# Delta rule: where three steps stand in the order of a pair of heads

## The reference, cut to what matters

```
conv = silu(conv1d(q, k, v))                    # 4 taps, per channel
decay = exp(tril(g_i - g_j))                    # g: sums of the gates in the chunk
tri = tril(k_beta @ k.T * decay, -1)
Tm = inverse(eye + tri)
v_new = Tm @ v_beta;  k_cum = Tm @ (k_beta * exp(g))
# over the chunks, one after the other:
v_n = v_new - k_cum @ S
out = q * exp(g) @ S + (q @ k.T * decay) @ v_n
S = S * exp(g_last) + (k * exp(g_last - g)).T @ v_n
# then per head
h = rmsnorm(out) * norm_weight * silu(z);  y = h @ W_out
```

## Time and profile before

| | before |
|---|---|
| median of the runs shown | 3314.37 us |
| the profiled execution, its own time | 3316.07 us |
| its span, first to last instruction | 3314.3 us |
| PE / weight load / VectorE / ScalarE / GpSimd busy | 91 / 63 / 70 / 37 / 31% |
| mean granted TensorE clock | 0.96 of full speed |

### The profile page before, as it was taken

The page is one execution under the profiler, slowest core; times in us unless marked ns, Lnnn a source line. Parts: engine busy times, 40 slices in busy tenths (PEclk is TensorE's granted clock), DMA queues, the critical chain, the costliest instruction groups (busy, mean ns, idle before and its releaser), DMA issues. The chain is left out here.

```text
span 3314.3 us, 81973 instructions
## 1 busy us (share of the span) xinstructions
PE 3003.8 (91%) x33019; PEld 2075.3 (63%) x33019; DVE 2307.2 (70%) x5231; ACT 1222.2 (37%) x2943; POOL 1022.4 (31%) x1495
## 2 busy tenths in 40 slices
PE   6999999599987999989999989999999999998897
PEld 3444444256655677677667767767776776776565
DVE  4666677778865776776776776777677677676466
ACT  2343333233333433343343343344344334332354
POOL 2454555348852221222221221221222122121011
PEclk8999999699988999999999999999999999998899
DMA  2111111000011110010010010000001001000000
GB/s 80 40 51 33 33 29 33 14 1 1 1 28 29 43 34 18 18 31 21 17 31 18 21 31 18 21 23 26 21 18 30 18 21 30 18 18 2 2 26 26
DMA packets 94040, 80.43 MB, mean 24 GB/s; under 512 B 54992, under 2 KB 68320, under 8 KB 93664
## 3 DMA queue, kind: packets, MB, share of 16 engines
q1 hardware_dynamic: 93664, 75.18, 8.4%
HBM read 57.70 MB, written 4.85 MB: 19 GB/s over the span
## 5 line engine op out<-in xcount | busy, mean ns | idle before, releaser
L1814 PE MATMUL gd_bk<-gd_xT,gd_wh 128*128 128x512 f32 x768 | 398.1, 628 | 22.1 <-DVE gd_L L1582 14.2
L480 DVE TENSOR_REDUCE at_nm<-at_ring 128x2 f32<-128x256 f32 (+3 forms) x256 | 199.2, 820 | 144.6 <-PE at_ring L623 144.6
L1528 DVE SCALAR_TENSOR_TENSOR gd_YK<-gd_bk,gd_cw,gd_YK 128x511 f32<-128x511 f32 (+2 forms) x384 | 282.8, 742 | 11.8 <-ACT gd_YK L1401 6.2
L1586 DVE COPY_PREDICATED gd_U<-gd_mU,gd_bk 128x256 f32<-128x256 int32 x320 | 140.9, 442 | 209.3 <-PE gd_bk L2016 149.5
L1994 PE MATMUL gd_bk<-gd_L,gd_NT 64*64 64x64 f32 x5120 | 212.5, 225 | 64.0 <-DVE gd_L L1588 41.3
L2011 PE MATMUL gd_bk<-gd_U,gd_ZS 64*64 64x64 f32 x5120 | 211.3, 225 | 39.4 <-ACT gd_ZS L1494 39.3
L1483 ACT COPY gd_O<-gd_bk 64x128 f32<-64x128 f32 x448 | 108.6, 260 | 356.9 <-PE gd_bk L1952 355.9
L1994 PEld LDWEIGHTS gd_bk<-gd_L,gd_NT 64*64 64x64 f32 x5120 | 177.9, 137 | 97.4 <-DVE gd_L L1588 55.8
L1494 ACT COPY gd_ZS<-gd_bk 128x256 f32<-128x256 f32 x320 | 115.2, 370 | 328.2 <-PE gd_bk L1994 324.9
L2011 PEld LDWEIGHTS gd_bk<-gd_U,gd_ZS 64*64 64x64 f32 x5120 | 178.4, 138 | 85.4 <-ACT gd_ZS L1494 43.5
L302 POOL TENSOR_TENSOR at_PT<-at_PT,at_dm 128x1024 f32<-128x1024 f32 (+3 forms) x128 | 198.0, 1547 | 10.7
(11 more groups left out here) (353 smaller groups left out, 6922.2 us busy)
## 6 DMA issues: line engine op xcount, KB each, us to landing
gd_wh<-in_L_attn_W_qkvz SPq DMA_DIRECT2D x64, 512.0 KB, 3.6
gd_gb<-gates SPq DMA_DIRECT2D x128, 64.0 KB, 3.3
X<-in_L_attn_x SPq DMA_DIRECT2D x8, 512.0 KB, 8.7
at_QT<-at_QS SPq DMA_DIRECT2D x128, 32.0 KB, 2.0
at_KT<-at_KS SPq DMA_DIRECT2D x128, 32.0 KB, 2.0
at_OC<-at_Ob SPq DMA_DIRECT2D x128, 32.0 KB, 2.0
at_RC<-inverse SPq DMA_DIRECT2D x128, 32.0 KB, 1.8
out_x<-X SPq DMA_DIRECT2D x8, 512.0 KB, 2.9
```

What stands on the lines that cost most here:

```text
L480: nc.vector.tensor_reduce(nm[v % 2][:, k, c0:c0 + HS + 1:HS], set_of(s, 2 + p)[:, :, 0:n], AX.X, ALU.max).then_inc(max_done, 1)
L1528: nc.vector.scalar_tensor_tensor(out[:, s:W], bank_[:, 0:W - s], cw[:, j, head(f, e), CONVK - 1 - s:CONVK - s], out[:, s:W], ALU.mult, ALU ...
L1586: last = nc.vector.copy_predicated(U[e][:, :, :], wide(mU[l]), chunks(A_[e], 1))
L1814: ins = nc.tensor.matmul(out[:, :], wh[e][:, k, col * DK:(col + 1) * DK], xT[:, k, :], start=k == 0, stop=k == DC - 1)
```

## The change

Seven moves and one new instruction in `delta_rule`; nothing else is changed.

1. ScalarE: `decays` of both heads go from level 1 to step 5, behind the first tap of head 0's values. A new Silu of one column (`warm`) stands in step 6 behind the copies to O and ahead of the squares. The first tap of head 1's values goes from step 6 to step 7.
2. GpSimd: `exponents(f + 1)` goes ahead of the gate weights (now a function of their own) and the key scales.
3. VectorE: head 1's first masked level in step 7 stands ahead of the output additions, in a new `front_middle`.
4. PE: the query projection of head 0 goes from the end of step 7 to step 8, behind the output products.
5. VectorE: the scalings of the outputs go from level 2, one behind each head's copies, to level 3, both ahead of the copies; the query taps of head 1 from level 3 to level 4.
6. PE and ScalarE: the heads' transposes and copies go from level 3 to level 4, `queries_out` of head 1 from level 4 to level 5; the values' transposes from level 4 to level 3.
7. PE: the output projection, four parts, goes from levels 4 and 5 to level 5 (one part) and behind it (three).

```diff
--- before.py
+++ after.py
@@ -973,6 +973,7 @@
         mL = [sb(f"mL{l}", [P, CK], I32) for l in range(LEVELS - 1)]
         xT = sb("xT", [P, DC, W])
         mhalf = sb("mhalf", [P, 2 * TPS])
+        warm = sb("warm", [P, 1])
         gates = nc.dram_tensor("gates", (NT * H, P), F32, kind="Internal").ap()
         glast = nc.dram_tensor("glast", (NT * H, CPT), F32, kind="Internal").ap()
         bk = [[bank(f"bk{e}{i}") for i in range(4)] for e in E2]
@@ -1308,6 +1309,8 @@
                         ge(pool, kc_mm[e], f)
                         nc.gpsimd.tensor_copy(U[e][:, :, :], wide(identc))
                         nc.gpsimd.tensor_copy(L[e][:, :, :], wide(identc)).then_inc(ui_done[e], 1)
+                def gate_weights(f):
+
                     for e in E2:
                         pool.wait_ge(z_silu[e], f + 1)
                         nc.gpsimd.tensor_tensor(zz[e][f % 2][:, :, :], zz[e][f % 2][:, :, :],
@@ -1382,9 +1385,11 @@
                     f = q + 1
                     if has(f):
                         prepare(f)
-                        key_scales(f)
                     if has(f + 1):
                         exponents(f + 1)
+                    if has(f):
+                        gate_weights(f)
+                        key_scales(f)
                     if ends_seq(q - 1):
                         row_scales(seq(q - 1))
                     if has(q):
@@ -1462,8 +1467,13 @@
                     if n == 3:
                         keys_out(f, 1)
                         gate_out(f, 1)
-                    if n in (5, 6):
-                        values_first(f, n - 5)
+                    if n == 5:
+                        values_first(f, 0)
+                        if has(f + 1):
+                            decays(f + 1, 0)
+                            decays(f + 1, 1)
+                    if n == 7:
+                        values_first(f, 1)
                     if n == 8:
                         queries_first(f, 0)
 
@@ -1481,6 +1491,8 @@
                                 act.wait_ge(p1_mm[e], q * RS + m)
                                 ge(act, ht_mm[e], q)
                                 nc.scalar.copy(O[e][rows(c), t, :], A_[e][rows(1 - c), 0:DK]).then_inc(o1_done[e], 1)
+                        if has(f) and n == 6:
+                            nc.scalar.activation(warm[:, :], mhalf[:, 0:1], ACT.Silu)
                         if has(q) and n >= 2 and n % 2 == 0:
                             squares(q, 0, n // 2 - 1)
                         if has(q) and n >= 2 and n % 2 == 0:
@@ -1494,18 +1506,15 @@
                                 nc.scalar.copy(ZS[e][:, :, :], chunks(A_[e])).then_inc(zs_done[e], 1)
                         if l == 1 and has(f):
                             queries_first(f, 1)
-                            if has(f + 1):
-                                decays(f + 1, 0)
-                                decays(f + 1, 1)
                             values_out(f, 0)
                         if l == 2 and has(f):
                             values_out(f, 1)
-                        if l == 3 and has(q):
+                        if l == 3 and has(f):
+                            queries_out(f, 0)
+                        if l == 4 and has(q):
                             heads_out(q, 0)
                             heads_out(q, 1)
-                        if l == 3 and has(f):
-                            queries_out(f, 0)
-                        if l == 4 and has(f):
+                        if l == 5 and has(f):
                             queries_out(f, 1)
                         if l == 5 and ends_seq(f) and has(f + 1):
                             act.wait_ge(xt_mm, DC * (seq(f) + 1) + 1)
@@ -1694,6 +1703,10 @@
                     if n == 7:
                         first_level(f, 0)
 
+                def front_middle(f, n):
+                    if n == 7:
+                        first_level(f, 1)
+
                 def front_late(f, n):
                     if n == 0:
                         keys_tap(f, 0, 1)
@@ -1711,8 +1724,6 @@
                         lower(f, 0)
                     if n == 6:
                         values_tap(f, 0, 1)
-                    if n == 7:
-                        first_level(f, 1)
                     if n == 8:
                         values_tap(f, 0, 2)
                         values_tap(f, 0, 3)
@@ -1747,6 +1758,8 @@
                                         dve.wait_ge(egl_in, 16)
                                     nc.vector.scalar_tensor_tensor(S[e][:, :], S[e][:, :], egl_row[:, col:col + 1], A_[e][:, DK:2 * DK],
                                                                    ALU.mult, ALU.add).then_inc(s_done[e], 1)
+                        if has(f):
+                            front_middle(f, n)
                         for e in E2:
                             m = n
                             if has(q) and 0 <= m < NCH and m % CPT == CPT - 1:
@@ -1770,7 +1783,10 @@
                         if l == 2 and has(f):
                             for s in range(1, CONVK):
                                 queries_tap(f, 0, s)
-                        if l == 3 and has(f):
+                        if l == 3 and has(q):
+                            heads_scaled(q, 0)
+                            heads_scaled(q, 1)
+                        if l == 4 and has(f):
                             for s in range(1, CONVK):
                                 queries_tap(f, 1, s)
                         if l == 5 and has(f):
@@ -1779,8 +1795,6 @@
                         for e in E2:
                             if has(f):
                                 level(f, e, l)
-                            if l == 2 and has(q):
-                                heads_scaled(q, e)
                         if l in (4, 5):
                             n = 2 * (f - FIRST_TERN) + l - 4
                             if 0 <= n < FSTEPS + PSTEPS:
@@ -1919,6 +1933,8 @@
                         values_in(f, 1, 1)
                     if n == 7:
                         lower_across(f, 1)
+                    if n == 8:
+                        queries_in(f, 0)
 
                 def front_late(f, n):
                     if n == 0:
@@ -1937,8 +1953,6 @@
                         values_in(f, 1, 0)
                     if n == 6:
                         lower_across(f, 0)
-                    if n == 7:
-                        queries_in(f, 0)
 
                 x_in(0, 0)
                 x_in(0, 1)
@@ -1996,13 +2010,13 @@
                                 last.then_inc(z_mm[e], 1)
                         if l == 1 and has(f):
                             queries_in(f, 1)
-                        if l == 3 and has(q):
+                        if l == 3 and has(f):
+                            values_across(f, 0)
+                        if l == 4 and has(q):
                             heads_across(q, 0)
                             heads_across(q, 1)
-                        if l == 4 and has(f):
-                            values_across(f, 0)
-                        if l >= 4 and ends_seq(q):
-                            project_out(seq(q), 2 * l - 8)
+                        if l == 5 and ends_seq(q):
+                            project_out(seq(q), 0)
                         for e in E2:
                             if has(f):
                                 pe.wait_ge(zs_done[e], f * (LEVELS - 1) + l)
@@ -2016,10 +2030,11 @@
                                             last = nc.tensor.matmul(A_[e][rows(c), t * CK:(t + 1) * CK], U[e][rows(c), t, :], ZS[e][rows(c), t, :],
                                                                     start=True, stop=True)
                                 last.then_inc(y_mm[e], 1)
-                        if l == 4 and has(f):
+                        if l == 3 and has(f):
                             values_across(f, 1)
-                        if l >= 4 and ends_seq(q):
-                            project_out(seq(q), 2 * l - 7)
+                        if l == 5 and ends_seq(q):
+                            for t in range(1, TPS):
+                                project_out(seq(q), t)
                     if ends_seq(f) and has(f + 1):
                         for e in E2:
                             ge(pe, ht_out[e], q + 1)
```

## The result

| | before | after |
|---|---|---|
| median of the runs | 3314.35 us | 3192.78 us |
| lowest to highest | 3314.29 to 3314.68 | 3184.38 to 3195.21 |
| the profiled execution | 3316.07 us, span 3314.3 | 3194.53 us, span 3192.8 |
| mean granted TensorE clock | 0.96 | 0.965 |

The ratio is 0.963, with an interval from 0.9614 to 0.9645: 121.6 us faster, where 100 were forecast. The direction and the mechanism hold, but the size was forecast too small. The changed kernel also spreads over 11 us between its runs, the one before over 0.4 us here.

A forecast was written before the change was run, and what follows sets the result against it. PE bounds the kernel, so only its waits can go: 23 ordinary pairs 75.9, seven sequence starts 20.3, with first and last pairs 99.7 us, giving 3214 us; own range 3195 to 3232, wide range 3192 to 3248 (0.80).

The forecast's parts named there:

- What bounds the kernel: PE, busy 3003.8 of 3314.3 us; only its waits can go, 115.4 us in four kinds around the inverse's levels.
- The exponentials in step 5: ScalarE: load and exponentials, 2.02 us, fit step 5 with 0.6 us spare; second load behind step 6's copies; cost nothing.
- the drain of the Trainium skill: ScalarE's table switches: 1.38 us drain atop 1283 ns, 2.66 us a switch; by it some 57 us above the forecast sum.
- GpSimd and the transfers: GpSimd's mask and G additions go ahead of gate weights, ending near 1831.1, about 17 us earlier; nothing lost.
- The rival on the slower side: Exponentials reach step 5 before their input, delaying ScalarE's copies and the recurrence; 25 us lateness gives 3491 us; chance 0.03.
- The rival of costlier switches: ScalarE's loads each hold it 2.57 us, making step 6's and 7's copies late: 52 us back, 3266; chance 0.03.
- The first masked level: VectorE does head 1's before the output additions in step 7; PE's waits of 0.45 and 0.71 us go.
- The levels, followed anew: Retimed levels 1 to 5 of one pair: 3.3 of PE's 4.12 us of waits go, 0.8 stay.
- The sum's check from totals: PE's four wait kinds, 115.4 us, less 0.8 for each of 32 pairs, is 90; some 10 us more missing there.
- The clock: Granted clock in the delta rule, mean 0.98: 10 us possible each way, none taken.
- VectorE as the bound: Rival: scalings and taps ahead of the level copies expose 1.13 us a pair, 34 us: 3248; chance 0.12.
- No change: Rival: PE's waits are only handed on to what ends last in the recurrence: 3314; chance 0.02.

The follow-up runs named there:

- the third kernel: Only the moves within the levels (scalings, query taps, transposes and copies, output projection), on the kernel before: 3293.7 us, ratio 0.9937.

## Why the prediction was right and wrong, point by point

- *What bounds the kernel.* Right: PE's brackets in front of the levels went, VectorE's and ScalarE's busy times are nearly what they were (2307.4 and 1235.1 us for 2307.2 and 1222.2), and the time followed.
- *The exponentials in step 5.* Right to a hundredth in ScalarE's slack; the drain of the Trainium skill (ScalarE: Activation LUTs, "What ACT_TABLE_LOAD costs") shows in none of these rows. That nothing in step 6 has to be protected by the small Silu, I had not seen: I costed it at nothing, and it brings nothing either.
- *GpSimd and the transfers.* Right: 17 us of slack, 16 forecast. (By the rows their start moves from 1848.25 to 1828.42, 20 us; the 17 that I wrote is counted from their new end.) The rival on the slower side was a real mechanism, and GpSimd's new order is what keeps it away. Its price for transfers 25 us late was not put to the test. The rival of costlier switches, and the sum by the drain, add step 7's lateness to step 6's as I did for GpSimd's; by the run with its order undone they would be too dear as well, but neither was run.
- *The first masked level.* Right; 1.29 us where its brackets said 1.16.
- *The levels, followed anew.* **This step failed, in size.** It said 3.3 of 4.12 us; the waits that stay are the 0.8 foretold, and 3.60 went. I took a bracket for the whole price of a wait. A bracket begins at the modelled end of the matmuls before it. In the kernel before, level 1's products of head 0, held apart from head 1's by 0.71 us, last 0.63 us from 1919.99 and those of head 1 make the next instruction start 0.61 us on; without a wait between them both are over in 1.08 us (2162.49 to 2163.57), not 1.24. In level 2 the second product begins 0.52 us after the first did (2168.44 to 2168.96); with a wait it had to be 0.68 and the bracket. Each of these two places is worth some 0.16 us more than its bracket: the 0.3 us a round that were missing. The other places gave what their brackets said, 0.43 us for 0.45 ahead of the query projection and 0.71 for 0.67 in levels 3 to 5. My own times in that pair show the same step: level 2's second product was to start at 26.3, and the changed kernel's starts at what would be 26.0 there; the Gram products at 40.0, and it is 39.7. I also put a penalty of 0.4 us on the 7 rounds with the normalization; it was 0.05. In sum 110.0 - 98.2 = 11.8 us, and 0.2 more in the first round (1.65 for 1.45). Two lines of the kernel before, beside those of the earlier trace rows:

```profile
1919.99 0.63 PE L1994 MATMUL gd_bk<-gd_L,gd_NT 64*64 64x64 f32 x16
1921.94 1.98 PE L1814 MATMUL gd_bk<-gd_xT,gd_wh 128*128 128x512 f32 x4
```

- *The sum's check from totals* was right in form and could not show this, since it used the same brackets.
- *The clock.* **This step failed too:** "none taken", with 10 us either way. It was 5.1 us between the marks. The experiments show that such stretches follow waits of PE, so a change that removes waits was to be given some of it, not zero on the mean.
- *What was neither.* 0.9 us ahead of the delta rule and 3.8 behind it are spread in code that is the same. Terms: 99.7 + 11.8 + 0.2 + 5.1 + 4.7 = 121.5. Without that spread the gain would be some 117 us, still well above 100.
- *Rivals.* VectorE as the bound: not so, in the third kernel and in the whole. Costlier table switches: not so, by the 0.61 and 0.28 us left. No change: not so, though a part of one wait was handed on when the exponentials moved alone.
- *The range* was too narrow by its own reasons. Its lower end was to be all 4.12 us of the waits gone and a better clock. The first alone is 30 x 0.82 = 25 us below 3214, 3189, and the clock's 10 us would bring it to 3179; the 3195 that was written has no sum behind it. The 3192.78 lies inside what those reasons give.

## What to carry to other kernels

A wait's bracket in a timeline is not its price: measure from start to start across the place, with and without the wait. Here a wait between two groups of 64x64 matmuls that otherwise follow one another directly was worth 0.16 us more than its bracket, and the one ahead of the query projection was not. Remove waits in the order in which they end last, and try parts alone and in pairs: PE's wait of 1.45 us a round for ScalarE gave 1.26 when it went alone, the rest came back as waits for VectorE, and only with the second part did 0.27 more come through. And move an engine's rare work (a sequence's statistics) to where that engine waits for PE; it cost 1.6 us a time where PE waited for it, and up to 2.6 more through the clock. When times spread or a gain is larger than its waits, look for stretches of low clock, and compare the stretches of the program that the change doesn't touch: here they differed by up to 5 us from trace to trace.

## What the hardware showed that was not expected

- A stretch of low clock (the lowest window of 4 us shows 0.50) costs 1.3 to 2.6 us a time in the changed kernel and follows a wait of PE: present at 4 of 7 waits of 1.8 us, at 7 of 7 of 3.1 us, and nowhere in the kernel with the statistics in step 0, where PE waits 0.2 us in that place. Stretches of the changed kernel around two of the waits of 1.8 us, one without the fall (1316 to 1324) and one with it (1556 to 1568; columns as in the earlier trace rows):

```profile
1316.00:1324.00 8.00, 5.93 (x42) 3.12 (x40) 6.85 (x28) 5.12 (x12) 3.92 (x9) 1.00 0.00 0
1556.00:1560.00 4.00, 1.94 (x8) 0.86 (x6) 3.83 (x14) 2.75 (x5) 3.59 (x9) 1.00 0.00 0
1560.00:1564.00 4.00, 4.00 (x16) 2.07 (x14) 2.42 (x11) 1.18 (x3) 0.31 (x1) 0.57 0.00 0
1564.00:1568.00 4.00, 4.00 (x54) 3.17 (x54) 3.56 (x12) 2.58 (x9) 0.00 (x0) 1.00 0.01 2
```

  PE has nothing to wait for from 1560 to 1564 and does 16 matmuls at 0.57 of the clock; then it is back at the full one.

- Square ran behind Exp, and behind Silu, with no table load between them (the kernel without the small Silu has two loads a round, not four).
- The runs of the kernel with the statistics in step 0 spread over 2.4 us, those of the changed kernel over 11. That the stretches make the difference is not shown: they are four runs each, the kernel without the small Silu spreads over 3.9 us with the statistics in step 4, and the one with a stretch at each of 7 places over 0.4.
